# Attention of a two-layer block: two masks moved from TensorE to VectorE, sums inverted in a packed form

## What is computed

```python
q = (x @ wq).reshape(b, s, NH, HD)
k = (x @ wk).reshape(b, s, NKV, HD)
v = (x @ wv).reshape(b, s, NKV, HD)
scores = jnp.einsum('bihd,bjhd->bhij', q, k) * SCALE
scores = jnp.where(causal, scores, jnp.finfo(scores.dtype).min)
attn = jax.nn.softmax(scores, axis=-1)
out = jnp.einsum('bhij,bjhd->bihd', attn, v)
return out.reshape(b, s, NH * HD) @ wo
```

## Time and profile before

| What | Value |
|---|---|
| Median of 3 runs | 950.62 us (949.71 to 951.45) |
| The profiled execution | 952.0 us, its span 950.1 us |
| Attention loop, first scores to first output product | 83.9 to 293.4 us |
| PE busy in the span | 877.9 us, 92% |
| DVE busy | 693.6 us, 73% |
| ACT busy | 533.1 us, 56% |
| POOL busy | 189.5 us, 20% |
| Mean granted clock of PE | 0.976 of 2.4 GHz |

### The profile page before, as it was taken

The page is one execution under the profiler, slowest core; times in us unless marked ns, Lnnn a source line. Parts: engine busy times, 40 slices in busy tenths (PEclk is TensorE's granted clock), DMA queues, the critical chain, the costliest instruction groups (busy, mean ns, idle before and its releaser), DMA issues.

```text
span 950.1 us, 13799 instructions
## 1 busy us (share of the span) xinstructions
PE 877.9 (92%) x5224; PEld 693.3 (73%) x5224; DVE 693.6 (73%) x892; ACT 533.1 (56%) x707; POOL 189.5 (20%) x197
## 2 busy tenths in 40 slices
PE   2799999999988889898999999999988999999996
PEld 1567667666667668686888888788866888888885
DVE  3835698888888768778677777587887866667842
ACT  3313667657654434486666657477727766666830
POOL 3002555666557213300000000000040000000004
PEclk9798999999898999999999999999999999999998
DMA  9588565655535103105233333133312333332202
GB/s 309 171 243 152 67 109 69 113 101 66 103 78 179 34 12 105 51 22 147 83 106 103 102 99 113 46 105 95 111 45 67 111 104 97 99 101 67 67 1 89
DMA packets 40610, 93.59 MB, mean 99 GB/s; under 512 B 7000, under 2 KB 10072, under 8 KB 40544
## 3 DMA queue, kind: packets, MB, share of 16 engines
q1 hardware_dynamic: 36416, 87.35, 36.6%
q10 hardware_dynamic: 4128, 5.36, 1.7%
HBM read 77.98 MB, written 2.11 MB: 84 GB/s over the span
## 4 chain that ended last, share of the span: by engine, by line
PE 75%; DVE 9%; issue 5%; POOL 4%; ACT 3%; DMA 2%; SPq 1%; POOLq 0%; DVEq 0%; ACTq 0%
PE PS L1509 15%; PE PS L1510 14%; PE PS L1511 14%; PE PS L1815 5%; PE PS L1814 5%; PE PS L1813 5%; PE PS L1607 4%; PE PS L1639 2%; PE PS L1622 2%; DVE MX L1295 2%; POOL QS L731 2%; DMA WM<-in_WM 1%; POOL X L715 1%; PE PS L1531 1%; DVE ACC L1157 1%
## 5 line engine op out<-in xcount | busy, mean ns | idle before, releaser
L837 ACT ACTIVATE PL<-CODE 128x1024 f32<-128x1024 int32 x200 | 201.9, 1057 | 60.3 <-DVE ACC L1157 55.7
L1509 PE MATMUL PS<-HH,WRH 128*128 128x512 f32 x448 | 176.7, 394 | 11.2 <-DVE HL L1116 4.7
L1510 PE MATMUL PS<-HH,WRL 128*128 128x512 f32 x448 | 175.6, 392 | 0.0
L1511 PE MATMUL PS<-HL,WRH 128*128 128x512 f32 x448 | 175.6, 392 | 0.0
L715 POOL TENSOR_TENSOR X<-X,SCR 128x512 f32<-128x512 f32 x32 | 42.6, 1343 | 560.2 <-DVE SCR L1142 560.1
L1157 DVE SCALAR_TENSOR_TENSOR ACC<-PL,ACC 128x1024 f32<-128x1024 f32 x100 | 123.1, 1231 | 8.4
L879 ACT ACTIVATE PT<-PS 128x512 f32<-128x512 f32 x160 | 85.5, 602 | 67.3 <-PE PS L1622 45.1
L1295 DVE TENSOR_REDUCE MX<-PS 128x2 f32<-128x256 f32 (+3 forms) x128 | 100.5, 820 | 29.4 <-PE PS L1609 14.8
L1509 PEld LDWEIGHTS PS<-HH,WRH 128*128 128x128 f32 x448 | 84.9, 189 | 31.2 <-issue 6.3
L731 POOL TENSOR_TENSOR QS<-ident,MX 64x256 fp32r<-64x256 f32 x128 | 93.6, 732 | 66.6 <-DVE MX L1295 60.0
L1511 PEld LDWEIGHTS PS<-HL,WRH 128*128 128x128 f32 x448 | 84.8, 189 | 18.0
(11 more groups left out here) (225 smaller groups left out, 1528.2 us busy)
## 6 DMA issues: line engine op xcount, KB each, us to landing
CODE<-in_CODES SPq DMA_DIRECT2D x50, 512.0 KB, 3.5
SCALE<-in_SCALES SPq DMA_DIRECT2D x100, 256.0 KB, 4.0
WM<-in_WM SPq DMA_DIRECT2D x12, 1024.0 KB, 5.9
QS<-FH SPq DMA_DIRECT2D x32, 128.0 KB, 4.1
QS<-FL SPq DMA_DIRECT2D x32, 128.0 KB, 5.1
X<-in_X ACTq DMA_DIRECT2D x2, 1024.0 KB, 12.3
GAB<-gates SPq DMA_DIRECT2D x4, 512.0 KB, 3.8
out_x<-X ACTq DMA_DIRECT2D x8, 256.0 KB, 2.0
```

Source lines behind the costliest of these rows:

```text
L837: nc.scalar.activation(PL[:, n % 3], CODE[:, p % 2], ACT.Prelu, scale=scale, bias=bias, alpha=alpha).then_inc(s_plane, 1)
L1509: nc.tensor.matmul(dst, lh, rh, start=start and k == 0, stop=False)
L1510: nc.tensor.matmul(dst, ll, rh, start=False, stop=False)
L1511: ins = nc.tensor.matmul(dst, lh, rl, start=False, stop=stop and k == KC - 1)
```

## The change

- The causal mask of query blocks 0 and 1 is no longer added by PE. DVE does it with a `tensor_tensor_reduce` for each head, which adds a mask tile (`CMASK`) to the scores in PSUM and takes the maximum in one instruction; the program holds a second, small instruction after each, which writes the maximum out. In blocks 2 and 3 all is as before.
- The transposed scores run three units behind the scores, not two (`TURN`), and three buffers hold maxima (`MAXIMA`). The weighted values run in the same steps as before.
- The sums of six of the eight pairs of stacks are no longer swapped and inverted as 128 x 512. SP packs them by two transfers into a tile of 128 x 32 (`RC`), DVE inverts that nine units after the pair's last one, SP stores the inverses in DRAM by two transfers and spreads them by one into `DENS`, already swapped, and DVE divides nineteen units after the pair's last one. The last two pairs go the old way.
- DVE's additions of the odd stack are parted: the values in unit 4, the sums in unit 5, after the maxima of that unit.
- The decoding steps ride in units 1, 3 and 7 of 8, codes and scales of a piece are loaded at places of their own, ACT evaluates each curve five to seven units ahead of its sum, and POOL scales and adds in other units. The fold of the sixth piece stands behind ACT's loop.

```diff
-PIECES_AT = {0: (0, 1), 5: (2,), 8: (3,), 11: (4,), 14: (5,)}
+CODES_AT = {0: (0, 1), 4: (2,), 6: (3,), 9: (4,), 12: (5,)}
+SCALES_AT = {0: (0, 1), 6: (2,), 9: (3,), 13: (4,), 15: (5,)}
 STACKS = 3
+MAXIMA = 3
+TURN = 3
...
+ADDED_MASK = (0, 1)
+PACK_AT = {2 * pair + 5: pair for pair in range(B * PAIRS - 2)}
+SPREAD_AT = {min(2 * pair + 6, B * GROUPS - 1): pair for pair in range(B * PAIRS - 2)}
...
 def step_at(n):
-    slots = (2, 4, 6)
+    slots = (1, 3, 7)
...
-    return divmod(n // 8 * len(slots) + slots.index(n % 8), STEPS)
+    at = n // 8 * len(slots) + slots.index(n % 8) - 1
+    return divmod(at, STEPS) if at >= 0 else None
...
+        def pack_sums(sp, pair):
+            b, c = divmod(pair, PAIRS)
+            sp.wait_ge(s_odd, 2 * pair + 2)
+            if pair:
+                sp.wait_ge(s_rs, 32 * pair)
+            for u in range(2):
+                sp.dma_start(RC[64 * u:64 * u + 64], DEN[HD * u:P:2 * HD, c, b * S:(b + 1) * S]).then_inc(s_dn, 16)
+        def store_inverses(sp, pair):
+            sp.wait_ge(s_ri, pair + 1)
...
+                sp.dma_start(INV[:, 1 - u], RC[64 * u:64 * u + 64]).then_inc(s_rs, 16)
+        def spread_inverses(sp, pair):
+            sp.wait_ge(s_rs, 32 * (pair + 1))
...
+            sp.dma_start(DENS[:], INV.rearrange("h u s -> (h u) s").unsqueeze(1).to_broadcast([GROUPS, HD, S])
+                         ).then_inc(s_rb, 16)
...
             for n in range(B * GROUPS):
+                if n in PACK_AT:
+                    pack_sums(sp, PACK_AT[n])
+                if n - 1 in PACK_AT:
+                    store_inverses(sp, PACK_AT[n - 1])
                 load_stack(sp, n)
...
+                if n in SPREAD_AT:
+                    spread_inverses(sp, SPREAD_AT[n])
...
-                for p in PIECES_AT.get(n, ()):
-                    load_piece(sp, p)
+                for p in CODES_AT.get(n, ()):
+                    load_codes(sp, p)
+                for p in SCALES_AT.get(n, ()):
+                    load_scales(sp, p)
...
                     w = (n % TB + 1) * P
-                    nc.vector.reduce_max(MX[:, n % 2, 2 * pair:2 * pair + 2], PS[:, 2 * pair:2 * pair + 2, 0:w], AX_X
+                    if n % TB in ADDED_MASK:
...
+                        for h in (2 * pair, 2 * pair + 1):
+                            ins = nc.vector.tensor_tensor_reduce(PS[:, h, 0:w], PS[:, h, 0:w], CMASK[:, TB * P - w:], 1.0,
+                                                                 MASKED, ALU.add, ALU.max, MX[:, n % MAXIMA, h:h + 1])
+                        ins.then_inc(s_mx, 1)
+                        continue
+                    nc.vector.reduce_max(MX[:, n % MAXIMA, 2 * pair:2 * pair + 2], PS[:, 2 * pair:2 * pair + 2, 0:w], AX_X
                                          ).then_inc(s_mx, 1)
...
                 if pair_at(n, 4) is not None:
-                    copy_odd(pair_at(n, 4))
+                    add_odd_values(pair_at(n, 4))
                 if pair_at(n, 5) is not None:
-                    swap_sums(pair_at(n, 5))
...
+                    add_odd_sums(pair_at(n, 5))
+                if pair_at(n, 8) in PACK_AT.values():
+                    invert_packed(pair_at(n, 8))
+                if pair_at(n, 18) in range(B * PAIRS - 3):
+                    divide(pair_at(n, 18))
+                if n == B * GROUPS * TB - 2:
+                    divide(B * PAIRS - 3)
+                    swap_sums(B * PAIRS - 2)
+                    invert(0)
+                if n == B * GROUPS * TB - 1:
+                    invert(1)
+                    divide(B * PAIRS - 2)
...
-                        nc.tensor.matmul(PS[:, h, ic * P:(ic + 1) * P], identR, maskR[:], start=False, stop=True,
...
+                        if ic not in ADDED_MASK:
+                            ins = nc.tensor.matmul(PS[:, h, ic * P:(ic + 1) * P], identR, maskR[:], start=False, stop=True,
+                                                   skip_group_check=True)
...
-            for n in range(units + 4):
+            for n in range(units + TURN + 1):
                 if n < units:
                     scores(n)
-                if 2 <= n < units + 2:
-                    transposed(n - 2)
+                if TURN <= n < units + TURN:
+                    transposed(n - TURN)
```

More of the change, by code:

```diff
@@ L860, in ride @@
             def ride(n):
-                if step_at(n) and step_at(n)[1] < STEPS - 1:
-                    curves(*step_at(n))
+                if step_at(n + 7) and step_at(n + 7)[1] == 0:
+                    curve(step_at(n + 7)[0], 0)
+                for ahead in (5, 6):
+                    if step_at(n + ahead) and ((n + ahead) % 8 == 1) == (ahead == 6) and step_at(n + ahead)[1] < STEPS - 1:
+                        p, s = step_at(n + ahead)
+                        curve(p, s + 1)
+                if step_at(n + 1) and step_at(n + 1)[1] == STEPS - 1:
+                    fold(step_at(n + 1)[0])
             act.wait_ge(s_const, 16 * 3)
@@ L867, in _ @@
             act.wait_ge(s_free, J["gsum",] + 1)
-            for n in range(3):
+            for n in range(-7, 0):
                 ride(n)
@@ L1318, in _ @@
                 split_heads(pair)
-            copy_odd(last)
+            add_odd_values(last)
+            add_odd_sums(last)
             swap_sums(last)
```

68 lines of the change are left out of this document (45 added, 23 removed).

## The result

The changed kernel takes **960.34 us** (median of 4 runs, 958.05 to 961.29) against 950.38 us for the kernel before: a ratio of 1.0093 with a 95% interval of 1.0066 to 1.0120. So it is slower by 0.9%. I had forecast 947.7 us; the time lies in my range (944 to 962), but the sign is wrong. The profiled execution took 961.29 us with a span of 959.5 us, 9.4 us more than before.

What follows compares the result with a forecast made beforehand. PE was taken to lead, with DVE almost as loaded. 952.0 - 7.3 (loop) + 4.3 (end) = 949.0 us profiled, 1.4 less for the median: 947.7 us; own range 946 to 948.7, eight in ten 944 to 962.

Steps and rivals of the forecast that it cites:

- the floor of the transfers: SP's issuing in the loop: 147 us from stack 3 to 15, so unit 60 not before 257.5.
- my 261.2: Forecast start of unit 60 in us, with the loop gaining 7.3 us.
- half a sentence of a rival: Loop gains only 3 to 6 us, possibly from DVE waiting for packed sums; end costs 4.3; 949 to 952, chance 0.20.
- if DVE waits for transfers: One of the signs listed beforehand that would show the forecast wrong; no size given.
- SP decides: Loop meets the floor of transfers at 257.5 to 259.5, gaining 9 to 11 us; 943.9 to 945.9, chance 0.16.
- my 949.0: Forecast time in us for the profiled kind of execution; the median was put 1.4 us lower.
- The masks: Blocks 0 and 1: PE saves 0.9 us a stack; four masked maxima cost DVE 1.6 and 2.1 us.
- Where the additions stand: Each pair, PE waits some 3.3 us, about 2.2 at the weighted values; a pair takes 24.1 us against 25.1.
- The sums: Packing takes 4.2 us a pair off DVE, adds a 0.2 to 0.4 us reciprocal; its issues cost SP 1.6 a stack.
- The end: Unit 60 to first output product: later WO load makes it 28.9 us against 24.9, plus 0.3 for clock; 4.3 us lost.
- The clock: Rival: the clock falls behind the new wait in each pair; 958.5 for four of seven, 966.6 for all; chance 0.30.
- Masked maxima at half rate: Rival: each element costs DVE 2.1 ns, 17 us in seven pairs, 964.5; chance 0.08.

Runs made afterwards that it cites:

- the run with the packing first: Changed kernel with a pair's two packing transfers issued on SP's queue before the earlier pair's spreading, the codes and the scales; 958.42 us.
- the run with the transfers on ACT: Changed kernel with the five packing, storing and spreading transfers of a pair issued by ACT instead of SP; 947.71 us.
- The early load of WO: Changed kernel with WO's load waiting for the last curve that reads the codes instead of the last curve sum; 953.01 us.
- the fastest kernel: Changed kernel with five transfers on ACT, both additions in one unit, gates' values behind unit 5, decoding one slot earlier, early WO load; 932.90 us.

## Why the prediction was wrong

**The step that failed** is the floor of the transfers. I wrote that SP needs 12.4 us a stack and that unit 60 could not start before 257.5, below my 261.2. The price was right (12.5). The start was wrong: I took 99 us for the fourth stack although I had written, two sentences on, that stacks are loaded one step later; it was 105.05. The row of twelve took 150.1 us, not 147, and the last stack had landed 10.9 us after its start (I said 11.5), at 266.07. So the floor was 266.1 and not 257.5, 8.6 us later, and above my forecast of the loop. Of the 6 us at the start 3.6 go when the gates' values come later (101.4; the kernel before had 100.0): a wait of PE that I had not looked at. In the run with the packing first PE starts each stack from the eighth on when it lands, and unit 60 at 269.01, 0.04 us after the last landing: there the floor is all there is.

Unit 60 of the changed kernel came 2.7 us after its own floor, and the second part of the step says why. DVE stood 11.2 us for the packed sums, behind which PE waited 4.2 and 3.2 us, the second time up to 236.91, so that the last three stacks came late without waiting for their own loads. I had priced that at nothing, apart from half a sentence of a rival, and had named "if DVE waits for transfers" as a sign of being wrong. So the rival "SP decides" was the case, but I had priced it as a gain, 943.9 to 945.9.

For the profiled execution, 961.3 against my 949.0, the 12.3 us are, but for rounding: unit 60 at 268.8 and not 261.2 (7.6), the end of the loop 0.5, and all that lies behind it 4.3 (2.0, 1.8 and 0.6), which I had put at nothing.

**The masks.** DVE's price was overestimated. Masked maxima follow each other at 0.25 us for 128 elements and 0.38 for 256 (starts at 154.00 and 154.25, 161.05 and 161.43), with the small second instruction inside: 1.0 and 1.5 us for four, not 1.6 and 2.1. PE's saving of 0.9 us a stack was overestimated too. It showed as 0.5 in the calm stack where no addition is waited for (10.50 against 10.98) and as nothing in the other (11.73 against 11.66), where the wait for the second addition is 1.3 us instead of 0.6: 0.4 us a pair.

**Where the additions stand.** The wait was where I put it, once in each pair, but 1.3 us at the weighted values, not 2.2 (3.3 with what I had added at the maxima): PE was ready 6.8 us after the step began (I said 6.3), DVE at 8.1 (I said 9.6), from the cheaper maxima. So calm pairs took 22.2 us, not 24.1. Had SP kept up, the loop would have been 4.7 us shorter than I forecast, as the run with the transfers on ACT shows (164.0 us against my 168.7).

**The sums.** Off DVE 4.2 us a pair was right in size; without packing a pair takes 3.4 us more. The packed reciprocal takes 0.35 us, near my upper bound of 0.4. Its five issues I had priced at 1.6 us a stack, rightly (1.24, 1.23 and 0.66 us a pair, and the gaps), but had not asked who queues on the other side: DVE stands in its order for a transfer, with the maxima behind it.

**The end.** 28.9 + 0.3 = 29.2 us forecast, 29.7 measured. The early load of WO confirms the cause. That the late fold would be hidden by the output products was wrong: it moved POOL's subtraction onto DVE's division, 3.2 us longer. Before the next stage's first product PE was idle for 2.9 us instead of 1.6, and the clock fell right behind that (327.34), as it had not before.

**The clock.** Behind the seven waits of 1.3 us it never fell. In the loop it fell behind the waits of 4.2 and 3.2 us (10.2 us at 0.50 in all) and behind the one of 3.4 us in the first stack (98.65 to 102.06). The length of one wait does not decide it alone: with the packing first it fell behind waits of 2.4, 2.0, 1.7 and 2.3 us and not behind one of 1.9, and the fall of the earlier trace rows came behind a wait of 1.2 us. What I had taken from the page of the Trainium skill, a lowered clock in every turn, was not borne out by waits of 1.3 us; the loop on that page, in "TensorE: Matmul & The Clock Gate", section "HAM oscillation — how this bites in real kernels", has longer waits than these.

**Masked maxima at half rate**: no; 0.13 us more for 128 elements more is one element in 1.0 ns, near the 1.04 that I took from the plain maxima.

## What to carry to other kernels

Before moving work into transfers, add up what the issuing queue already does per turn, from its first start to its last landing: if the sum comes near the turn, each small transfer costs its full issue time, whether or not anyone waits for it. Compute such a floor from the start that the changed order gives, since an error there moves the end with it. The same edit can have another sign under another limit (the masks on DVE: 7 us lost with the packing on SP's queue, 3 us gained by the medians with it on ACT's), so measure pairs of edits. And before an edit gets the credit for a gain, compare stage by stage: of the 9.9 us that came with the additions together, 2.8 were in the loop.

## What the runs showed that was not expected

- An issue of 8 KB costs SP about as much as one of 128 KB, 0.6 to 0.7 us, and up to 1.3 us behind others; 27 of them cost 16 us of a kernel's time.
- A stack's same twelve issues took SP 9.7 us with the masks on DVE and 9.3 with the masks on PE; with the transfers on ACT 10.1 and 9.6, in the fastest kernel 10.0 and 9.6. But it is no rule of the masks: the kernel before, with the masks on PE, has 9.8. Open why.
- A tensor_tensor of DVE with both sources in SBUF took 3.9 and 4.75 us instead of 0.70 beside one long instruction of POOL. Whether three such instructions at the end met it or not made 5 us of the output stage, between kernels that differ little.
- The masked maximum with its accumulator read costs 0.25 us for 128 elements and 0.38 for 256 when queued, less than a reduction of the same 256 elements (0.42 us) although it takes two instructions.
